# Feed-forward phases with features on partitions and 512 tokens a unit; maximum over keys by a 32x32 transpose and a reduce

## The reference

```python
for l in range(2):
    h = shift_token(x)                       # second half of the features comes from the token before
    q, k, v = split(h @ wqkv[l])             # 8 heads of 64
    q = l2norm(q) * q_scale; k = l2norm(k) * k_scale
    q, k = rotary_xpos(q, k)                 # tables of 512 tokens x 64
    x = x + local_attention(q * 8, k, v) @ wo    # windows of 64, own window and the one before
    h = layernorm(shift_token(x)) * ln_g + ln_b
    a, g = split(h @ w1 + b1)                # 341 each
    x = x + (a * gelu(g)) @ w2 + b2
```

## Time and profile before

| | |
|---|---|
| median of 3 runs | 2400.47 us (2398.17 to 2400.76) |
| the profiled execution, its own time | 2398.42 us |
| its span in the trace | 2396.6 us |
| PE, DVE, ACT, POOL busy, of the span | 88%, 91%, 70%, 52% |
| mean granted TensorE clock | 0.975 |

### The profile page before, as it was taken

The page is one execution under the profiler, slowest core; times in us unless marked ns, Lnnn a source line. Parts: engine busy times, 40 slices in busy tenths (PEclk is TensorE's granted clock), DMA queues, the critical chain, the costliest instruction groups (busy, mean ns, idle before and its releaser), DMA issues. The chain is left out here.

```text
span 2396.6 us, 58054 instructions
## 1 busy us (share of the span) xinstructions
PE 2115.1 (88%) x20074; PEld 1660.4 (69%) x20074; DVE 2178.8 (91%) x5128; ACT 1672.6 (70%) x3681; POOL 1235.7 (52%) x1036
## 2 busy tenths in 40 slices
PE   2888899889888888799999996999888898888888
PEld 2677777777777777466666664777777777777776
DVE  4999999999999999688888887999999999999997
ACT  1677666776677667488888894667667676767665
POOL 3665556655656555222232225565655665565553
PEclk9999999999999999899999998999999999999999
DMA  3000000000000000000000000000000000000000
GB/s 109 2 2 1 2 2 2 2 1 2 2 2 2 1 2 2 1 2 2 1 2 1 2 2 1 1 2 1 2 1 2 2 2 6 6 6 6 6 6 11
DMA packets 12756, 12.35 MB, mean 5 GB/s; under 512 B 1413, under 2 KB 11703, under 8 KB 12471
## 3 DMA queue, kind: packets, MB, share of 16 engines
q1 hardware_dynamic: 12471, 8.63, 1.2%
HBM read 6.53 MB, written 2.10 MB: 4 GB/s over the span
## 5 line engine op out<-in xcount | busy, mean ns | idle before, releaser
L849 POOL TENSOR_TENSOR RN<-SS,mhalf 128x16 f32<-128x16 f32 x128 | 373.8, 2921 | 9.5 <-DVE SS L723 9.4
L840 POOL TENSOR_TENSOR U2B<-U,b_s 128x128 f32<-128x128 f32 x128 | 61.7, 482 | 584.3 <-DVE U L729 577.1
L541 ACT ACTIVATE PR<-bank,NMX 128x128 f32<-128x128 f32 x1024 | 290.1, 372 | 49.2 <-DVE NMX L634 45.6
L598 ACT ACTIVATE GL<-bank,b_s 114x128 f32<-114x128 f32 (+1 forms) x384 | 113.2, 366 | 258.0 <-PE bank L388 258.0
L379 PE MATMUL bank<-KT,QZ 128*64 128x128 f32 x4096 | 280.1, 279 | 0.0
L379 PEld LDWEIGHTS bank<-KT,QZ 128*64 128x64 f32 x4096 | 218.3, 136 | 70.2 <-issue 70.2
L1094 ACT ACTIVATE PL<-bank,NM 128x384 f32<-128x384 f32 (+3 forms) x512 | 255.8, 540 | 14.2 <-DVE NM L1172 11.4
L1172 DVE TENSOR_REDUCE NM<-bank 128x1 f32<-128x384 f32 (+3 forms) x352 | 217.6, 634 | 35.6 <-PE bank L1008 31.7
L388 PE MATMUL bank<-HN,w_s 128*114 128x128 f32 (+1 forms) x1536 | 222.0, 281 | 0.0
L1017 PE MATMUL bank<-cst,PL 128*128 128x128 f32 x1280 | 199.7, 275 | 3.2 <-DVE PTL L1181 1.1
L364 PE MATMUL bank<-wqkv_h,HTH 128*128 128x512 f32 x384 | 194.7, 507 | 5.7 <-DVE HTL L709 5.7
(11 more groups left out here) (158 smaller groups left out, 6230.8 us busy)
## 6 DMA issues: line engine op xcount, KB each, us to landing
X<-in_L_attn_x SPq DMA_DIRECT2D x8, 256.0 KB, 4.6
out<-X SPq DMA_DIRECT2D x8, 256.0 KB, 2.3
wqkv_raw<-in_L_ffn_wqkv SPq DMA_DIRECT2D x1, 1536.0 KB
w_s<-in_L_ffn_w SPq DMA_DIRECT2D x1, 682.0 KB
rope<-shape_constants SPq DMA_DIRECT2D x1, 512.0 KB
wo_s<-in_L_ffn_wo SPq DMA_DIRECT2D x2, 256.0 KB
cst<-shape_constants SPq DMA_DIRECT2D x1, 259.0 KB
w_s<-in_L_ffn_w SPq DMA_DIRECT2D x2, 114.0 KB
```

The source lines that it names most:

```text
L541: last = nc.scalar.activation(PR[:, 4 * g + h, :], BK[B_S[g]][:, h * P:(h + 1) * P], ACT.Exp, bias=NMX[:, 4 * g + h:4 * g + h + 1], scale=8.0)
L849: nc.gpsimd.tensor_tensor(RN[:, u % 2, :], SS[:, :], mhalf[:, 0:2 * NH], ALU.pow).then_inc(S["rn_ok"], 1)
```

## The change

A unit of `ffn_phase` is now one sequence of **512 tokens** of a layer, with **features on partitions**: 2 x 8 = 16 units a phase. The residual stream lives transposed in tile Z. Weights are the stationary operand, the 512 tokens stream.

- q and k come in four blocks m (query and key of two groups g of four heads), each as two halves z of 32 features a head, so that 128 partitions hold 4 heads x 32. `rotate` on DVE multiplies one half with both tables in one instruction of 1024 elements; POOL subtracts and adds (`rotate`). The sums of squares are a product with `hsum`; ACT takes Ln and Exp(-0.5 x) of them, DVE refines the result in three instructions (`norms`), and SP writes it to DRAM and reads it back spread over partitions in four DMAs. POOL multiplies it onto q and k (`norms`, 1024 elements, four a unit).
- `scores` puts keys on partitions and queries on the free axis: per group g, four masks of 128x512 and 64 float32 products of 32 rows and 64 columns; the four heads i lie in four row groups and write to four banks.
- The maximum over keys is over partitions now. Per head DVE transposes the bank in 32x32 blocks and reduces (`maxima`); PE turns the 64 results (`turn_max`), DVE reduces again and spreads them (`spread_max`), and PE adds minus the maximum to the banks by a product of 512 columns (`add_max`). It is one maximum for 32 queries and not for each query. ACT then takes exp, 512 columns an instruction, and writes the operand of the next product as it is: the transposes of probabilities, of q, k and of the result are gone.
- The sums of exp are a product with ones; ACT makes 1/x with Ln and Exp(-x); SP spreads it through DRAM; `attended` multiplies. The second layernorm's factor goes the same way. v for the other window parity is copied by DMA. The product with w1 is split in three float32r products.
- In the setup the rotation tables are no longer multiplied with the scales; w1 is split in two halves.

```diff
-c = NMX[:, 4 * g:4 * g + 4]
-link(nc.vector.tensor_reduce(c, BK[B_S[g]][:, :].rearrange("p (h q) -> p h q", h=4),
-                             AX_X, ALU.max))
-nc.vector.tensor_scalar(c, c, -8.0, None, ALU.mult).then_inc(S[("nmx0_ok", "nmx1_ok")[g]], 1)
 ...
-nc.vector.tensor_tensor(RA[:, u % 2, g, :, :], src,
-                        ropet[:, l, t, 2 * g, :].unsqueeze(1).to_broadcast([P, NH, DH]),
-                        ALU.mult)
-tab = ropet[:, l, t, 2 * g + 1, :].rearrange("p (z d) -> p z d", z=2)
-nc.vector.tensor_tensor(
-    RB[:, g, :, :].rearrange("p h (z d) -> p h z d", z=2), rot,
-    tab.unsqueeze(1).to_broadcast([P, NH, 2, DH // 2]),
-    ALU.mult).then_inc(S[("qmul", "kmul")[g]], 1)
 ...
-                NU = DEPTH * NS
+                NU = DEPTH * NB
 ...
+def norms(u):
+    sp.wait_ge(S["nw_ok"], u + 1)
+    sp.dma_start(norms_d[u % 2], RN[0:P:8, :]).then_inc(S["r_out"], 16)
+    sp.wait_ge(S["r_out"], 16 * (u + 1))
+    if u >= 1:
+        sp.wait_ge(S["nr_ok"], 4 * u)
+    for i in range(4):
+        src = norms_d[u % 2].rearrange("(c i) n -> i c n", i=4)[i]
+        sp.dma_start(SQ[32 * i:32 * i + 32, :, 1, :],
+                     src.unsqueeze(0).broadcast_to([32, 4, T])).then_inc(S["r_in"], 16)
 ...
+def sums(u, g):
+    n = 2 * u + g
+    sp.wait_ge(S["dl_ok"], n + 1)
+    sp.dma_start(sums_d[n % 2], DR[0:P:32, :]).then_inc(S["d_out"], 16)
+    sp.wait_ge(S["d_out"], 16 * (n + 1))
+    if u >= 1:
+        sp.wait_ge(S["wo_in"], u)
+    for e in range(2):
+        src = sums_d[n % 2].rearrange("(j e) n -> e j n", e=2)[e]
+        sp.dma_start(OT[W * e:W * e + W, 2 * g:2 * g + 2, :],
+                     src.unsqueeze(0).broadcast_to([W, 2, T])).then_inc(S[("d0_in", "d1_in")[g]], 16)
 ...
+for n in range(-2, NU + 5):
+    run(result, n - 5)
+    run(sums, n - 1, 0)
+    run(sums, n - 1, 1)
+    run(norms, n)
+    run(variances, n - 2)
+    run(values, n)
 ...
+def project(u, m):
+    l = u // NB
+    pe.wait_ge(S["htl_ok"], u + 1)
+    claim(4, "na_ok", 4 * u + m + 1)
+    claim(5, "sb_ok", 4 * u + m + 1)
+    g, e = divmod(m, 2)
+    for z in range(2):
+        o = ((e * 2 + g) * 2 + z) * P
+        for k, (w, h) in enumerate(((wqkv_h, HTH), (wqkv_h, HTL), (wqkv_l, HTH))):
+            last = nc.tensor.matmul(BK[4 + z][:, :], w[:, l, o:o + P].bitcast(F32R), h[:, :].bitcast(F32R),
+                                    start=(k == 0), stop=(k == 2))
+    last.then_inc(S["pr_in"], 1)
 ...
+def scores(u, g):
+    pe.wait_ge(S["nr_ok"], 4 * u + 2 * g + 2)
+    for i in range(4):
+        claim(i, "ex_ok", 8 * u + 4 * g + i + 1)
+        nc.tensor.matmul(BK[i][:, :], identb[:, :], bandb[:, :], start=True, stop=False,
+                         skip_group_check=True)
+    for t in range(NT):
+        for z in range(2):
+            for e in range(2):
+                k0 = (2 * t + e) * W
+                n = min(2 * W, T - k0)
+                for i in range(4):
+                    r = slice(32 * i, 32 * i + 32)
+                    last = nc.tensor.matmul(
+                        BK[i][e * W:(e + 1) * W, k0:k0 + n], QK[r, 2 * g + 1, z, k0:k0 + W],
+                        QK[r, 2 * g, z, k0:k0 + n], start=False, stop=(z == 1),
+                        skip_group_check=True)
+    last.then_inc(S["s_in"], 1)
+
+def turn_max(u, g, k):
+    pe.wait_ge(S["mx_ok"], 8 * u + 4 * g + 4)
+    claim(k, "cb_ok", 2 * u + g + 1)
+    pe.transpose(BK[k][0:64, 0:P], MX[:, :, :], ident).then_inc(S["mt_in"], 1)
+
+def add_max(u, g):
+    pe.wait_ge(S["cb_ok"], 2 * u + g + 1)
+    for i in range(4):
+        nc.tensor.matmul(BK[i][:, :], pick[:, i:i + 1].to_broadcast([64, P]).bitcast(F32R),
+                         CB[:, :, :].rearrange("p a b -> p (a b)").bitcast(F32R), start=False, stop=True,
+                         skip_group_check=True).then_inc(S["ca_in"], 1)
 ...
+pe.wait_ge(S["preset"], PRESETS)
+for n in range(-2, NU + 5):
+    run(hidden, n - 4, 0, 1, 7)
+    run(project, n, 0)
+    run(hidden, n - 4, 0, 2, 6)
+    run(scores, n - 1, 0)
+    run(outward, n - 4, 6)
+    run(turn_max, n - 1, 0, 7)
+    run(project, n, 1)
+    run(add_max, n - 1, 0)
+    run(join, n - 2, 7)
+    run(project, n, 2)
+    run(scores, n - 1, 1)
+    run(sums, n - 1, 0, 7)
+    run(project, n, 3)
+    run(turn_max, n - 1, 1, 6)
+    run(center, n - 2, 7)
+    run(add_max, n - 1, 1)
+    run(norms, n, 6)
+    run(variance, n - 2, 5)
+    run(attend, n - 1, 0, 7)
+    run(sums, n - 1, 1, 4)
+    run(hidden, n - 3, 1, 0, 6)
+    run(attend, n - 1, 1, 7)
+    run(hidden, n - 3, 1, 1, 5)
+    run(hidden, n - 3, 1, 2, 4)
+    run(attend, n - 1, 2, 7)
+    run(attend, n - 1, 3, 6)
+    run(values, n, 0, 5)
+    run(values, n, 1, 4)
+    run(values, n, 2, 5)
+    run(values, n, 3, 7)
+    run(hidden, n - 3, 0, 0, 4)
+    run(tokens, n + 1, 6)
+    run(back, n - 4, 6)
 ...
+def norms(u):
+    link(nc.scalar.activation(RN[:, :], VN[:, :], ACT.Ln))
+    nc.scalar.activation(RN[:, :], RN[:, :], ACT.Exp, scale=-0.5).then_inc(S["rl_ok"], 1)
 ...
+        act.wait_ge(S["d_out"], 16 * n)
+    nc.scalar.activation(DR[:, :], BK[k][:, :], ACT.Ln).then_inc(S["dn_ok"], 1)
+    act.wait_ge(S["dn_ok"], n + 1)
+    nc.scalar.activation(DR[:, :], DR[:, :], ACT.Exp, scale=-1.0).then_inc(S["dl_ok"], 1)
 ...
+for n in range(-2, NU + 5):
+    run(values, n - 1, 2, 5)
+    run(high, n)
+    run(values, n - 1, 3, 7)
+    run(square_a, n, 0)
+    run(square_b, n, 0)
+    run(square_a, n, 1)
+    run(softmax_exp, n - 1, 0)
+    run(square_b, n, 1)
+    run(square_a, n, 2)
+    run(square_b, n, 2)
+    run(sums, n - 1, 0, 7)
+    run(square_a, n, 3)
+    run(high_hidden, n - 3)
+    run(square_b, n, 3)
+    run(square_c, n - 2, 7)
+    run(softmax_exp, n - 1, 1)
+    run(norms, n)
+    run(sums, n - 1, 1, 4)
+    run(gate, n - 3, 0, 6)
+    run(gate, n - 3, 1, 5)
+    run(gate, n - 3, 2, 4)
+    run(variance, n - 2)
+    run(values, n, 0, 5)
+    run(values, n, 1, 4)
 ...
+    o = 2 * (1 - z)
+    nc.vector.scalar_tensor_tensor(
+        out=TP[:, o:o + 2, :], in0=BK[4 + z][:, :].unsqueeze(1).to_broadcast([P, 2, T]), scalar=q,
+        in1=tab[:, e, :, :], op0=ALU.mult, op1=ALU.mult).then_inc(S[("na_ok", "nb_ok")[z]], 1)
 ...
+def maxima(u, g):
+    for i in range(4):
+        link(nc.vector.transpose(NT_[:, :], BK[i][:, :]))
+        nc.vector.tensor_reduce(MX[:, i, :], NT_[:, :].rearrange("p (a b) -> p a b", b=32),
+                                AX_X, ALU.max).then_inc(S["mx_ok"], 1)
+        dve.wait_ge(S["mx_ok"], 4 * n + i + 1)
 ...
+    link(nc.vector.tensor_reduce(CT[:, :], BK[k][0:64, 0:P].rearrange("p (a i) -> p i a", a=4),
+                                 AX_X, ALU.max, negate=True))
+    if n >= 1:
+        dve.wait_ge(S["ca_in"], 4 * n)
+    nc.vector.tensor_tensor(CB[:, :, :].bitcast(F32R), CT[:, :].unsqueeze(1).to_broadcast([64, 16, 32]),
+                            place[:, :].unsqueeze(2).to_broadcast([64, 16, 32]),
+                            ALU.mult).then_inc(S["cb_ok"], 1)
 ...
+for n in range(-2, NU + 5):
+    run(statistics, n + 2)
+    run(gated, n - 4, 1, 7)
+    run(rotate, n, 0, 1)
+    run(gated, n - 4, 2, 6)
+    run(rotate, n, 0, 0)
+    run(maxima, n - 1, 0)
+    run(spread_max, n - 1, 0, 7)
+    run(rotate, n, 1, 1)
+    run(rotate, n, 1, 0)
+    run(outward, n - 4, 6)
+    run(residual, n - 2, 7)
+    run(rotate, n, 2, 1)
+    run(rotate, n, 2, 0)
+    run(maxima, n - 1, 1)
+    run(rotate, n, 3, 1)
+    run(spread_max, n - 1, 1, 6)
+    run(rotate, n, 3, 0)
+    run(clamp, n, 6)
+    run(attended, n - 1, 0, 7)
+    run(add_eps, n - 2, 5)
+    run(norms, n)
+    run(attended, n - 1, 1, 7)
+    run(attended, n - 1, 2, 7)
+    run(attended, n - 1, 3, 6)
+    run(variance, n - 2)
+    run(gated, n - 3, 0, 4)
+    run(arrive, n + 1, 6)
+    run(tokens, n + 2)
+    run(back, n - 4, 6)
 ...
+def low(u):
+    pool.wait_ge(S["hth_ok"], u + 1)
+    nc.gpsimd.tensor_tensor(HTL[:, :].bitcast(F32R), Z[:, u % NB, 0:T], HTH[:, :],
+                            ALU.subtract).then_inc(S["htl_ok"], 1)
+
+def rotate(u, m):
+    pool.wait_ge(S["na_ok"], 4 * u + m + 1)
+    pool.wait_ge(S["nb_ok"], 4 * u + m + 1)
+    if u >= 1:
+        pool.wait_ge(S["s_in"], 2 * (u - 1) + m // 2 + 1)
+    nc.gpsimd.tensor_tensor(QK[:, m, 0, :], TP[:, 2, :], TP[:, 1, :], ALU.subtract)
+    nc.gpsimd.tensor_tensor(QK[:, m, 1, :], TP[:, 0, :], TP[:, 3, :], ALU.add).then_inc(S["ad_ok"], 1)
+
+def norms(u, m):
+    pool.wait_ge(S["ad_ok"], 4 * u + m + 1)
+    pool.wait_ge(S["r_in"], 64 * (u + 1))
+    nc.gpsimd.tensor_tensor(QK[:, m, :, :], QK[:, m, :, :],
+                            SQ[:, m, 1, :].unsqueeze(1).to_broadcast([P, 2, T]),
+                            ALU.mult).then_inc(S["nr_ok"], 1)
 ...
+for n in range(-2, NU + 5):
+    run(tokens, n + 2)
+    run(low, n)
+    run(norms, n - 1, 1)
+    run(norms, n - 1, 2)
+    run(norms, n - 1, 3)
+    run(rotate, n, 0)
+    run(hidden, n - 3)
+    run(rotate, n, 1)
+    run(rotate, n, 2)
+    run(low_hidden, n - 3)
```

(25 more changed lines are left out.)

966 lines of the change are left out of this document (410 added, 556 removed).

## The result

The changed kernel takes **2814.57 us** (median of 4 runs, 2800.82 to 2821.61) against 2399.32 us (2397.47 to 2400.76) for the kernel before in the same comparison: a ratio of **1.172**, 95% interval 1.168 to 1.177. That is slower, as forecast, but by 415 us and not by 90; it lies outside the range of 2340 to 2640. The profiled execution took 2821.61 us, its span is 2819.8 us, its mean granted TensorE clock 0.822 (0.975 before).

A forecast was written before the change was run, and what follows sets the result against it. No engine but a chain through all of them, closed by the norms' DRAM trip, was to set a 57.4 us step; a phase of 114 + 15 x 57.4 = 975 us, +90 in all, gave 2490 us, range 2340 to 2640.

The forecast's parts named there:

- step 8: SP's queue: sums' trip, then the norms' write (2.2 us) and four reads through DRAM, from 43.7 to 53.5 us.
- step 9: POOL's norms product, 2.5 us, then its low half, 1.3, which releases PE's next projection at 57.4 us.
- Step 3: DVE's first maxima of a step, 5.6 us, to 13.0, with each transpose taken at 0.68 us.
- rival "DVE": Slower: transpose takes 1.2 us, step 61.6, 2616 us; or a lower TensorE clock of the same size; together chance 0.15.
- Step 7: DVE's clamp, then ACT's Ln and Exp of norms and sums with a table load at each function change, to 43.7 us.
- faster, by tables: Exp and Ln share one ACT table, three loads leave the chain: 3.9 us, step 53.5, 2373 us; chance 0.13.
- the drain at each switch: Slower: a drain of 1.4 us at each ACT table switch of the chain, 2655 us; chance 0.02.
- Step 2: First scores on PE: masks 0.95 us, then 128 records at 0.03, 3.7 us, ending with draining at 7.4.
- faster, by row groups: All eight score tiles run side by side on PE: 1.7 us instead of 3.7, step 53.4, 2370 us; chance 0.20.
- Steps 1, 4 and 6: PE's projection (1.5 us), first add_max and join (to 20.6), second add_max and norms product (to 36.1).
- The second chain: PE's late products wait for banks that ACT empties behind its table loads; PE is through at about 55.6 us.
- The ramp: Start and end of a phase beyond 15 full steps: 114 us, including about 30 before the first unit's first scores.

The follow-up runs named there:

- PE kept at work: Changed kernel plus bf16 products nobody reads on PE, 18 before the first projection and 12 before each turn of the maxima: 2638.4 us.

## Why the prediction was right in direction and wrong in size

**Right.** The steady part stopped being bound by an engine, and a loop through all of them took over (DVE 427 of 800 us, PE 568). It closes where step 8 and step 9 had it: Exp of the sums before SP's write of the norms, POOL's product waiting for that DMA, PE's first projection waiting for POOL's low half. Also as forecast are the nine table loads a step, DVE at 35 us and PE at 47 a step (427 and 568 of 800, times 65.7), and the setup, 4 us longer (DVE's first statistics at 46.03 instead of 42.11). Step 3's price of the transpose, 0.68, measured 0.716, so of the rival "DVE" the half on the transpose falls; its other half, the lower clock, came true. Step 7 had 7.6 us from the clamp's start to the end of the sums' Exp, and it is 7.2 (610.88 to 618.03). The rivals "faster, by tables" and the drain at each switch fall by ACT's timeline: a load before each function, and the function 0.01 us behind the load.

**Step 2 was too dear.** I took 0.03 us a record from L478, 4.8 with the masks. Measured are 2.8. The rule of the Trainium skill (TensorEngine Tiling (Array Packing), Tiling Modes), that tiles of 32 rows and 64 columns work eight at a time, holds in this trace: 128 records in 2.03 us, near my lower bound of 1.7. So the condition of the rival "faster, by row groups" came true and brought the 4 us a step that it was priced at, and the kernel was still slower, since other terms grew by more.

**Steps 1, 4 and 6 were priced at full clock.** This is the first failed step. I had the row (0.70 where PE is busy for 60% of a stretch), I wrote that PE would stand still for 12 to 16 us of a step, and yet I left the clock in a rival that shared a chance of 0.15, with 4.2 us. In the step from 605.17 us on (64.9 us long), the first projection took 2.5 instead of 1.5, two `add_max` 2.07 instead of 1.0, `join` 5.3 instead of 3.4, the norms product 3.6 instead of 1.9: +6.7. A second projection, which the walk had beside the spreading of the maxima, took 2.3 instead of 1.5, in part at the lower level, and `add_max` in PE's queue behind it started 2.4 us after the maxima instead of 1.3: +1.1. Less 4.0 on the scores and plus 0.5 on the maxima, that gives the 4.3 us by which the norms product ends later than in the walk (40.4 against 36.1). With PE kept at work the step is 5.8 us shorter. The forecast should have contained the lower level in every product that follows a wait.

**Step 8 was too cheap.** From the sums' Exp to the norms in POOL's hands I had 9.8 us and it is 13.7. The write of the norms took 3.6 instead of 2.2 behind the sums' reads, the reads 7.0 instead of 4.4. The earlier trace rows have a first use 2.9 us after an issue of 256 KB; I let the last of four reads land 2.9 us after its start. The four need 7.03 us behind other DMAs and 7.19 in the first unit with nothing ahead, 1 MB at about 150 GB/s and not at 296. So what was wrong is the time of the reads themselves, not what stands ahead of them. The Trainium skill (DMA: Bandwidth & Descriptors, Latency and other measured facts) has the memory's access latency rise from 0.2 to 2 us at high load; the norms' write, 1.83 us in the first unit and 3.63 behind 512 KB of reads, is in line with that, and so are the 3.16 us of the sums' write on a queue of its own. How much of the growth is load and how much place in the queue no run here settles. The remark that taking the trip away "would bring 2 us" was low as well: 5.7, since the trip was longer by 3.9. The second chain grew from 55.6 to 60.0 us, about the 4.3 that both chains share.

**The ramp was 41 us short a phase.** I summed 30 us before the first scores, without a working. It was 55.5 (50.4 to 105.9): up to the clamp alone 33.2 passed, and then the first unit too goes through ACT's loads, Ln and Exp, the norms' trip and POOL's product, 22.3 more. After the last unit's first scores there were 94.9 us (2719.55 to 2814.4) against 84. The last 4 us are that the 15 steps from scores to scores took a little longer than those from clamp to clamp. At the end of a phase the stages of the last unit, 512 tokens long, run with little beside them. The edits moved this term little: the last clamp to the end of the span is 127.1 us in the changed kernel and 118 to 127 in the others, so at most 9 us of a phase's ramp.

**The sum.** 8.3 us a step are 249 us, two ramps 82: 331 of the 334 us. Within the step of 64.9 us the lower clock adds 6.7 and the second projection 1.1, the trip 3.9, the maxima 0.5; the scores take 4.0 away, ACT's part 0.4 (step 7), and POOL's two products 0.3 (631.72 to 635.33, 3.6 instead of 3.9). That is its 7.5 us over the forecast. That the clock, the trip, the loads and the maxima lie on the loop was tried by taking each away (5.8, 5.7, 2.2 and 11 us a step); the first is a lower bound, since the clock came back to 0.94 and not to 1. The unread products did not stand in the way there: behind them PE still waited 0.65 and 0.82 us for the maxima and 2.44 for the low half. The scores' price, the size of the reads and the ramp were read from the trace, no run tried them.

## What to carry to other kernels

When a rewrite takes the load off every engine, price the loop: walk one step through all queues, and price at the lower clock level the matmuls that follow waits like these, of 3 to 5 us. Price a trip through DRAM by its bytes and by what is in flight at that time; two trips on one queue trade places when they are reordered. Count the ramp by walking the first and the last unit: a phase of the kernel before takes about 75 us beyond 15 times 57.1, the changed one 154.9, and this moved the point of balance from 57 to 51.6 us a step. Products that nobody reads help only where PE waits: the same 18 cost 3.6 us a step once their wait was gone.
